# Sharing a PSUM bank between heads on the causal diagonal: 128- and 256-column score units joined

## The reference

```
x = layernorm(x + windowed_attention(x))        # windows of 128, one head
x = layernorm(x + block(x))
block: q, k = rope(x) @ Wq, rope(x) @ Wk; v = x @ Wv     # 16 heads of 16
       scores = q k^T / 4, causal mask, softmax, @ v, output projection, layernorm
       gates = softmax(x1 @ gate_w); the top 2 of 8 experts, weighted; layernorm
```

## Time and profile before

| | |
|---|---|
| time of three runs | 1547.62, 1549.48, 1550.94 us (median 1549.48) |
| the profiled execution | 1549.67 us |
| its span, first to last instruction | 1547.9 us |
| mean granted TensorE clock | 0.974 |
| mx / st units, pv matmuls | 1280 / 1312 / 2624 |
| units of 128 / 256 / 384 / 512 columns | mx 128 / 128 / 128 / 896; st 144 / 176 / 112 / 880 |
| mask matmuls | 512 in mx, 512 in st |

### The profile page before, as it was taken

How to read it: one execution, slowest core, us unless ns; L and a number is a source line. 1 busy time by engine, 2 the same in 40 slices (tenths; PEclk the granted TensorE clock), 3 DMA queues, 4 the chain that set the end, 5 groups by cost and what they waited for, 6 DMA issues and landing times.

```text
span 1547.9 us, 27399 instructions
## 1 busy us (share of the span) xinstructions
PE 1455.6 (94%) x9264; PEld 764.6 (49%) x9264; DVE 1090.7 (70%) x2736; ACT 814.5 (53%) x1899; POOL 425.7 (28%) x704
## 2 busy tenths in 40 slices
PE   8889999999999999999999999998999979999677
PEld 6667755565444464453656554444443333343242
DVE  3667667678777887877755677777778877887135
ACT  3235345555556556646565546453665637556631
POOL 4335544232322231221424332322111101110114
PEclk9999999999999999999999999998999989999888
DMA  4745432124010230010217131113000000010000
GB/s 119 197 136 135 112 87 54 50 66 109 23 46 26 53 98 15 24 38 23 64 31 168 47 92 31 49 46 86 19 23 15 23 15 15 22 26 19 22 1 14
DMA packets 143369, 86.60 MB, mean 56 GB/s; under 512 B 106430, under 2 KB 136390, under 8 KB 142975
## 3 DMA queue, kind: packets, MB, share of 16 engines
q1 hardware_dynamic: 143231, 84.85, 21.4%
HBM read 58.76 MB, written 25.43 MB: 54 GB/s over the span
## 4 chain that ended last, share of the span: by engine, by line
PE 55%; DVE 5%; ACT 3%; issue 3%; POOL 1%; SPq 1%; DMA 1%; POOLq 0%; DVEq 0%; ACTq 0%
PE bank L1307 12%; PE bank L1418 11%; PE bank L1287 11%; PE bank L1261 9%; ACT pbuf L913 2%; DVE mxs L998 2%; PE bank L1377 1%; PE bank L1396 1%; SPq L741 1%; PE bank L1265 1%; DMA qs<-eb_nmT 1%; PE bank L1290 1%; PE bank L1413 1%; PE bank L1338 1%; PE bank L1344 1%
## 5 line engine op out<-in xcount | busy, mean ns | idle before, releaser
L998 DVE TENSOR_REDUCE mxs<-bank 128x1 f32<-128x512 f32 (+3 forms) x1280 | 729.6, 603 | 190.9 <-PE bank L1265 122.2
L913 ACT ACTIVATE pbuf<-bank 128x512 f32<-128x512 f32 (+3 forms) x1312 | 609.7, 533 | 337.7 <-PE bank L1307 173.9
L1287 PE MATMUL bank<-qs,ks 99*128 99x512 bf16 (+3 forms) x1312 | 446.6, 350 | 22.2 <-DMA qs<-eb_nmT 18.4
L1261 PE MATMUL bank<-ks,qs 96*128 96x512 bf16 (+3 forms) x1280 | 442.4, 353 | 4.8 <-DVE mxs L998 3.4
L1307 PE MATMUL bank<-pbuf,vcur 128*17 128x512 f32 (+3 forms) x2624 | 266.2, 523 | 10.3 <-ACT pbuf L913 9.9
L1287 PEld LDWEIGHTS bank<-qs,ks 99*128 99x128 bf16 x1312 | 129.9, 99 | 242.9 <-issue 137.2
L1418 PE MATMUL bank<-ew,x1T 128*128 128x512 f32 x464 | 228.0, 614 | 0.0
L1261 PEld LDWEIGHTS bank<-ks,qs 96*128 96x128 bf16 x1280 | 126.5, 99 | 144.7 <-issue 42.6
L1307 PEld LDWEIGHTS bank<-pbuf,vcur 128*17 128x17 f32 x2624 | 60.5, 97 | 142.6 <-issue 106.1
L1418 PEld LDWEIGHTS bank<-ew,x1T 128*128 128x128 f32 x464 | 82.9, 194 | 66.4 <-issue 62.4
L1290 PE MATMUL bank<-idb,maskb 128*128 128x128 bf16 x512 | 111.9, 220 | 0.0
(11 more groups left out here) (263 smaller groups left out, 1715.2 us busy)
## 6 DMA issues: line engine op xcount, KB each, us to landing
parts_scratch<-parts SPq DMA_DIRECT2D x29, 384.0 KB, 3.4
vcur<-v_scratch SPq DMA_DIRECT2D x80, 136.0 KB, 2.4
xw<-windows SPq DMA_DIRECT2D x29, 256.0 KB, 3.1
qs<-parts_scratch SPq DMA_DIRECT2D x32, 192.0 KB, 3.3
ks<-parts_scratch SPq DMA_DIRECT2D x32, 192.0 KB, 3.2
ks<-parts_scratch SPq DMA_DIRECT2D x32, 128.0 KB, 2.8
qs<-parts_scratch SPq DMA_DIRECT2D x32, 128.0 KB, 3.4
v_scratch<-vst SPq DMA_DIRECT2D x29, 136.0 KB, 1.8
```

Of the source, the lines that this page charges most:

```text
L913: nc.scalar.activation(pbuf[:, i % PB, r0:r1], bk[:, r0:r1], ACT.Exp)\
L998: v.reduce_max(mxs[:, j * HJ + h, c:c + 1], bk[:, 0:width], AX_X).then_inc(emptied[b], 1)
L1261: last = mm(bk[:, 0:width].rearrange("p (n t) -> p n t", t=P), qs5[0:KR, pos % QRING, j, head, :], ks5[0:KR, kslot, 0:width // P, head, :] ...
L1287: last = mm(bk[:, r0:r1].rearrange("p (n t) -> p n t", t=P), ks5[0:KR + NPART, kslot, kb % GT, head, :], qs5[0:KR + NPART, place(J) % QRIN ...
```

## The change

Four units of 128 columns (one for each head of the job) become one unit in one bank, and two units of 256 columns become one. For four heads one mask matmul comes first and writes the mask four times side by side (512 columns, its moving operand repeated by a stride of 0), then the four score matmuls add to it. For two heads each head's score and mask follow each other as before. One VectorE reduction now gives four or two maxima; one ScalarE exponential writes four or two slots of pbuf. Units of 384 and 512 columns stay. The waits of `pv` and `nm_a` are moved to the new last unit. The planner has new prices for TensorE: each matmul of a unit costs at least 98 ns, a mask 95 in place of 56, the mask of four heads 220; the ranks of a job's units run over the new, shorter lists.

```diff
+def heads_together(cols):
+    return HJ if cols == P else HJ // 2 if cols == 2 * P else 1
+@functools.lru_cache(None)
+def mx_list(J):
     s, hg, j0, nj = JOBS[J]
...
+    for c in range(keys_groups(J)):
+        for j in range(j0, j0 + nj):
+            cols = (j + 1) * P if c == s % GB else GQ
+            n = heads_together(cols)
+            out += [(c, j, h, n, cols) for h in range(0, HJ, n)]
+def st_list(J):
+    for kb in range(key_tiles(J)):
+        lo, hi = st_tiles(J, kb)
+        n = heads_together((hi - lo) * P)
+        out += [(kb, h, n, (hi - lo) * P) for h in range(0, HJ, n)]
+def st_last(J, kb):
+    return max(i for i, x in enumerate(st_list(J)) if x[0] <= kb)
...
-            rows["mx", J, i] = ("PE", cols / 2.4 + 3 + 56 * diag, r + length * i / n,
+            rows["mx", J, i] = ("PE", heads * max(cols / 2.4 + 3, 98) + (220 if cols == P else 95 * heads) * diag, r + length * i / n,
...
-            rows["mr", J, i] = "DVE", cols / 0.96 + 55, r + length * i / n, [("mx", J, i)] + ([("nm_a", J - 1)] if J else [])
+            rows["mr", J, i] = ("DVE", heads * cols / 0.96 + 55, r + length * i / n,
+                                [("mx", J, i)] + ([("nm_a", J - 1)] if J else []))
...
-            rows["st", J, i] = ("PE", cols / 2.4 + 3 + 56 * diag, r + length * i / n,
+            rows["st", J, i] = ("PE", heads * max(cols / 2.4 + 3, 98) + (220 if cols == P else 95 * heads) * diag, r + length * i / n,
...
-            rows["ex", J, i] = ("ACT", cols * 0.833 + 68, r + length * i / n,
+            rows["ex", J, i] = ("ACT", heads * cols * 0.833 + 68, r + length * i / n,
...
-            rows["pv", J, kb] = ("PE", cols * 4 / 2.4 + 34 + 95, r + length * (HJ * (kb + 2 - kb % 2) + 2) / n,
+            rows["pv", J, kb] = ("PE", cols * 4 / 2.4 + 34 + 95, r + length * (st_last(J, kb + 1 - kb % 2) + 1.5) / n,
...
-                    nc.scalar.activation(pbuf[:, i % PB, r0:r1], bk[:, r0:r1], ACT.Exp)\
+                    nc.scalar.activation(pbuf[:, u0:u0 + heads, nj * P - cols:nj * P],
+                                         bk[:, 0:heads * cols].rearrange("p (h t) -> p h t", h=heads), ACT.Exp)\
...
-                    v.reduce_max(mxs[:, j * HJ + h, c:c + 1], bk[:, 0:width], AX_X).then_inc(emptied[b], 1)
+                    v.reduce_max(mxs[:, j * HJ + h:j * HJ + h + heads, c],
+                                 bk[:, 0:heads * cols].rearrange("p (h t) -> p h t", h=heads), AX_X)\
...
+                    if heads == HJ:
+                        mm(bk[:, :].rearrange("p (h t) -> p h t", h=HJ), idb[:, :],
+                           maskb[:, :].unsqueeze(1).broadcast_to([P, HJ, P]), start=True, stop=False)
+                    for x in range(heads):
+                        head = hg * HJ + h + x
+                        last = mm(bk[:, x * cols:(x + 1) * cols].rearrange("p (n t) -> p n t", t=P),
+                                  qs5[0:KR, pos % QRING, j, head, :], ks5[0:KR, kslot, 0:cols // P, head, :],
+                                  start=heads < HJ, stop=x == HJ - 1 or not diag)
+                        if diag and heads < HJ:
+                            last = mm(bk[:, x * cols + j * P:x * cols + (j + 1) * P], idb[:, :], maskb[:, :],
+                                      start=False, stop=True)
...
+                    if heads == HJ:
+                        mm(bk[:, :].rearrange("p (h t) -> p h t", h=HJ), maskb[:, :],
+                           idb[:, :].unsqueeze(1).broadcast_to([P, HJ, P]), start=True, stop=False)
...
-                        pe.wait_ge(*drain("st", J, HJ * (kb + 2) - 1))
+                        pe.wait_ge(*drain("st", J, st_last(J, kb + 1)))
```

More of the change, by code:

```diff
@@ L992, in _ @@
                     J, i = step[1:]
-                    c, j, h, width = mx_at(J, i)
+                    c, j, h, heads, cols = mx_list(J)[i]
                     j -= JOBS[J][2]
@@ L1285, in _ @@
                         pe.wait_ge(nm_loaded, 16 * HJ * (J + 1))
-                    head, kslot = hg * HJ + h, ((s // GB) * GB + kb // GT) % KRING
-                    last = mm(bk[:, r0:r1].rearrange("p (n t) -> p n t", t=P), ks5[0:KR + NPART, kslot, kb % GT, head, :],
-                              qs5[0:KR + NPART, place(J) % QRING, lo:hi, head, :], start=True, stop=not diag)
-                    if diag:
-                        last = mm(bk[:, r0:r0 + P], maskb[:, :], idb[:, :], start=False, stop=True)
+                    kslot = ((s // GB) * GB + kb // GT) % KRING
+                    if heads == HJ:
+                        mm(bk[:, :].rearrange("p (h t) -> p h t", h=HJ), maskb[:, :],
+                           idb[:, :].unsqueeze(1).broadcast_to([P, HJ, P]), start=True, stop=False)
+                    for x in range(heads):
+                        head = hg * HJ + h + x
+                        last = mm(bk[:, x * cols:(x + 1) * cols].rearrange("p (n t) -> p n t", t=P),
+                                  ks5[0:KR + NPART, kslot, kb % GT, head, :],
+                                  qs5[0:KR + NPART, place(J) % QRING, lo:hi, head, :],
+                                  start=heads < HJ, stop=x == HJ - 1 or not diag)
+                        if diag and heads < HJ:
+                            last = mm(bk[:, x * cols:x * cols + P], maskb[:, :], idb[:, :], start=False, stop=True)
                     last.then_inc(filled[b], 1)
```

61 lines of the change are left out of this document (22 added, 39 removed).

## The result

| | before | after |
|---|---|---|
| median of the runs | 1548.82 us | 1494.48 us |
| lowest to highest | 1547.62 to 1550.94 | 1489.6 to 1497.64 |
| ratio, 95% interval | | 0.9645 [0.9616, 0.9674] |
| the profiled execution, its span | 1549.67, 1547.9 | 1494.53, 1492.7 |
| TensorE not busy (span less PE) | 92.3 us | 66.8 us |

The change takes 54 us off, 3.5%. The direction was one I gave 0.40, the size one I gave nothing.

A forecast was written before the change was run, and what follows sets the result against it. The prediction took TensorE's summed work to bound most of the run. Its terms, 0.8 + 0.3 + 1.5 + 0.2 = 2.8 us, came off 1549.5 to give 1546.7 us, with a range of 1537 to 1558.

The forecast's parts named there:

- I take zero for the new order: All queues' order from the planner's new prices: counted as no gain or loss, though prices were about 37 us too high.
- for most of the run the time is the sum of TensorE's work: Long stretches, TensorE 97 to 98% busy: other engines' work was said to count only in TensorE's gaps.
- Term (c): Score banks: joined units hold banks longer, no worse than 512-column units with three banks per kind; 0.2 us gained.
- term 1: TensorE's masks in 68 groups of four heads: one 512-column mask for four short ones saves 0.8 us.
- rival D: TensorE's joined mask: its repeated operand is slow, costing 15 us more, 1561 us; chance 0.03.
- VectorE and ScalarE: Fewer reductions and exponentials: 10 us or 24.6 by means, up to 15 or 32; counted as nothing beside TensorE's work.
- term (a): End of the last job: ScalarE's last exponentials become three units, 1.59 us in place of 1.89, 0.3 us less.
- Term (b): Ends of jobs: shorter diagonal reductions let the row maxima's chain finish earlier; 1.5 us gained, bounds 0 and 5.
- N: Whole kernel: all relief is hidden, only TensorE's 0.8 us and the tail's 0.3 show, 1548.4 us; chance 0.20.
- G: Ends of groups: a shorter chain or another order takes a third of TensorE's idle time, 12 us, 1537; chance 0.18.
- L: TensorE's short matmuls: each costs its weight load of 99 ns, so the change gains 12 us, 1537; chance 0.04.
- S: Ends of jobs: the overpriced diagonal makes TensorE wait, a third of 37 us becomes stalls, 1559 us; chance 0.20.

The follow-up runs named there:

- e2: Changed kernel's order, banks and semaphores, but each head in a joined unit has its own mask, reduction and exponential again; 0.9705 of the kernel before.
- e3: Changed kernel planned anew with the planner's old TensorE prices for score units; 0.9612 of the kernel before.
- e6: Changed kernel with filler (other layers' work) forced as early as in the kernel before or earlier; 1.0515 of the kernel before.
- e17: Kernel before, planned so that a set's units follow one another on TensorE, VectorE and ScalarE where possible, instructions unchanged; 0.9834 of the kernel before.
- e9: Kernel before, planned with no filler step on TensorE while a set of units is unfinished; 0.9911 of the kernel before.
- e1: Changed kernel's joined instructions in the order and banks of the kernel before; ratio 1.001 to the kernel before.
- e4: Kernel before with single units, planned anew with the changed kernel's TensorE prices for one head; 0.9831 of the kernel before.

## Why the prediction was wrong

**The step that failed** is "I take zero for the new order, with both ends from the idle time it could touch". All but the last 9 us of the gain are in it (e2), and its ends were far too near: the runs show 60 us less (e3, 0.0388 of 1549) to 80 us more (e6) for orders of nearly the same instructions. I had looked at the planner's prices only, and found them too high by 37 us. What I passed over is that a joined unit can't be split by any other step, where 332 of the 356 places inside the sets had one; this stands in the diff as plainly as the prices do. Forbidding the splits alone brings 26 us (e17), forbidding only those by filler 14 (e9). By what joined units gain the 20 us beyond e17 is open, so the step that failed is known, and its mechanism about by half.

**The reading under it** that failed: "for most of the run the time is the sum of TensorE's work". It was drawn from TensorE's 97 to 98% in the long stretches. I had written that "busy" hides short stalls, and then took a stretch of 98% for covered all the same. Counted by starts, stalls (slow matmuls at the lower clock among them) were 173 us before and are 126 now (e1: 174, e17: 146); only 92.3 us of the former span show as idle at all.

**Term (c), banks**: "in front of mx units TensorE waited only 3.4 us for VectorE". The same cause stands at the weight loads with 75 us. The group was on the list of groups; I read it for its 99 ns and not for its last column. The term was 0.2 us; the idle time of this kind at the weight loads fell by 37, most of it by the order, as e1 has 80.7 us of it and e2 41.7. The prediction also called the diagonal VectorE's densest part; at 0.63 busy against 0.81 it was the thinnest.

**The masks, term 1** (0.8 us): the joined mask's 512 columns take 0.22 us to the next start (399.73 to 399.95 above), the value I took; rival D is excluded. **VectorE and ScalarE**: I had bounds of 10 and 24.6 us, 15 and 32; the pages say 16.2 and 14.5 for the change and 8.6 and 19.4 for e1, which has the same instructions, so a busy sum tells such a saving only to some 8 us. A reduction with four results costs what one with one result does, and the long ones are what they were:

```profile
L1006 DVE TENSOR_REDUCE mxs<-bank 128x1 f32<-128x512 f32 x896 | 579.0, 682 | 130.5 <-PE bank L1277 105.1 <-PE bank L1281 24.6
...
L1006 DVE TENSOR_REDUCE mxs<-bank 128x2 f32<-128x512 f32 x64 | 43.6, 686 | 11.4 <-PE bank L1281 11.2
L1006 DVE TENSOR_REDUCE mxs<-bank 128x4 f32<-128x512 f32 x32 | 22.0, 687 | 9.3 <-PE bank L1277 9.2
```

That this relief is worth nearly nothing by itself was right as long as the order stays: e1 shows it.

**The tail, term (a)**: the last exponentials, three units now, take 1.70 us where I had 1.59 and before had 1.89:

```profile
1427.73 1.70 ACT L920 ACTIVATE pbuf<-bank 128x512 f32<-128x512 f32 x3 [1.23 <-PE bank L1329]
```

The two pairs and the quad don't run back to back, since the quad's mask is only issued 0.45 us after the first of them starts:

```profile
1428.18 0.39 PE L1303 MATMUL bank<-idb,maskb 128*128 128x512 bf16 x1
1428.40 0.39 PE L1307 MATMUL bank<-qs,ks 99*128 99x128 bf16 x4
```

So 0.2 us came of the 0.3. **Term (b)**, 1.5 us for ends of jobs: the waits it is about, of st units for the DMAs and at nm_T, add up to 25.1 us before, to 24.7 in e1, where only the relief is there, and to 20.4 in the changed kernel. So the relief brought 0.4 us of waits and the order the rest. Behind job 35's last unit nothing changed: TensorE is not busy for 16.6 us in both.

**The rivals.** N was right for what e1 tests, and wrong for the change. G had the right sign and half of the mechanism, that the order leaves filler in better places; but it looked for the gain at the ends of groups and priced it by their idle time, 12 us, where it lay in stalls in and between the diagonals that "busy" hides. L was given 0.04 for another reason and is refuted: in the changed kernel the four scores behind a quad's mask are again 0.055 us apart, less than their weight loads' 98 ns. S had the planner's too high prices cost time; single units gained 26 us by them (e4), and joined ones neither gained nor lost (e3). The rule that I set beside the rows there, some 81 ns for a pair of load and matmul at 128 columns (the Trainium skill, "TensorE: Matmul & The Clock Gate", section "Back-to-back issue gap"), would have given 7 us; by those 0.055 us and by e1 it does not hold here.

## What to carry to other kernels

Where a planner orders the queues, a change of what counts as one step is a change of order: count, in the order before, how often another step stands inside what the change joins (here 332 of 356 places), and look at that ahead of any instruction saved. Look for bank waits at the weight loads, and take TensorE's busy share for an upper bound only; starts against their usual distance tell more. Before shipping such a gain, try two or three other orders of the same instructions, for they scatter (here by some 16 us). The rule "finish a set before you begin something else" brought half of the gain here with no instruction changed, and so did higher prices on the diagonal; which of such rules helps was only found by running them.

## What the runs showed of the hardware that was not expected

- An operand repeated by a stride of 0 cost TensorE here what a plain one does: 512 columns of mask in 0.22 us to the next start (median of 68), as a score matmul of 512 columns. The mean of the rows (386 and 379 ns) is no longer than the 0.38 to 0.39 us of those:

```profile
L1303 PE MATMUL bank<-idb,maskb 128*128 128x512 bf16 x36 | 13.9, 386 | 0.0
...
L1273 PE MATMUL bank<-maskb,idb 128*128 128x512 bf16 x32 | 12.1, 379 | 0.0
```

- A reduction over 512 columns takes 682 ns with one result a partition, 686 with two and 687 with four (rows above).
- A wait of a score matmul for its bank is recorded at its weight load (75.2 us before) and only to a small part at the matmul (3.4 us in front of mx units, 2.6 in front of st units).
